# The tanh message-passing layer: gated vector products spread over three pipeline steps, with one more multiply on VectorE

## The reference, cut to what matters

```python
xs = concat([x[src, :8], x[dst, :8]])                   # 16 scalars of an edge
xv = concat([x[src, 8:], x[dst, 8:]]).reshape(E, 16, 3) # 16 vectors of an edge
h = sqrt(2) * relu(emb @ W1 / sqrt(10))
w = (h @ W2 / 4).reshape(E, 7, 16, 8)                   # per-edge weights
s_out, g_out = ...      # sums of xs and of the dots xv . n with w: 8 scalars, 8 gates
v_out = ...             # 8 vectors: xs x n with w, xv with w, and (xv, y2, W3J) with w
out = concat([1.593 * tanh(s_out), (1.593 * tanh(g_out))[:, :, None] * v_out]) * norm
return segment_sum(out, dst)
```

## Time and profile before

| | us |
|---|---|
| median of 3 runs | 14662.81 (14660.83 to 14662.97) |
| the profiled execution, its own time | 14665.89 |
| its span, first to last instruction | 14664.2 |
| PE busy in the span | 12078.2 (82%) |
| DVE busy | 12076.0 (82%) |
| POOL busy | 9995.6 (68%) |
| ACT busy | 7889.6 (54%) |

### The profile page before, as it was taken

The page is one execution under the profiler, slowest core; times in us unless marked ns, Lnnn a source line. Parts: engine busy times, 40 slices in busy tenths (PEclk is TensorE's granted clock), DMA queues, the critical chain, the costliest instruction groups (busy, mean ns, idle before and its releaser), DMA issues. The chain is left out here.

```text
span 14664.2 us, 437528 instructions
## 1 busy us (share of the span) xinstructions
PE 12078.2 (82%) x114342; PEld 9157.5 (62%) x114342; DVE 12076.0 (82%) x30182; ACT 7889.6 (54%) x23572; POOL 9995.6 (68%) x10550
## 2 busy tenths in 40 slices
PE   1555555555566999999999999988899999999999
PEld 1444444445455666666666666666677777777777
DVE  5777777777768999999999999986677777777776
ACT  0455555555544666666666666647544444444443
POOL 4777777777765666666666666637677777777775
PEclk8666666666668999999999999989899999999999
DMA  3555555555542222222222222218511111111111
GB/s 95 83 87 87 86 87 87 86 87 87 87 73 41 36 36 36 36 36 36 36 36 36 36 36 36 36 20 282 174 25 25 25 25 25 25 25 25 25 25 24
DMA packets 2705893, 840.24 MB, mean 57 GB/s; under 512 B 2232498, under 2 KB 2650073, under 8 KB 2704124
## 3 DMA queue, kind: packets, MB, share of 16 engines
q1 hardware_dynamic: 2212179, 616.76, 21.2%
q0 software_dynamic: 312320, 178.52, 9.3%
q10 hardware_dynamic: 181250, 43.25, 1.4%
HBM read 610.22 MB, written 226.58 MB: 57 GB/s over the span
## 5 line engine op out<-in xcount | busy, mean ns | idle before, releaser
L1401 POOL DMA_INDIRECT w_rows<-table,w_idx x9375 | 8949.5, 955 | 3848.0 <-issue 2539.0
L1384 PE MATMUL w_p_deg<-w_hot_lo,w_hot_row 128*128 128x196 bf16 x6250 | 1802.8, 336 | 1570.3 <-DVE w_hot_lo L1329 1512.1
L1637 PE MATMUL w_p_w<-w_w,w_ht 128*128 128x256 f32 x12500 | 3033.1, 390 | 0.0
L1637 PEld LDWEIGHTS w_p_w<-w_w,w_ht 128*128 128x128 f32 x12500 | 2272.7, 190 | 404.3 <-issue 0.2
L1869 DVE TENSOR_TENSOR w_prod<-w_p_xe,w_he 128x512 f32<-128x512 f32 x3125 | 2137.6, 684 | 4.1 <-PE w_p_xe L2012 4.1
L1619 ACT ACTIVATE w_ht<-w_p_h 128x512 f32<-128x512 f32 x1875 | 851.0, 526 | 2270.5 <-PE w_p_h L1651 2270.5
L1358 ACT CAST w_counts<-w_p_count 128x784 uint8<-128x784 f32 x1875 | 1247.7, 706 | 1451.8 <-PE w_p_count L1385 1442.0
L1384 PEld LDWEIGHTS w_p_deg<-w_hot_lo,w_hot_row 128*128 128x128 bf16 x6250 | 832.6, 133 | 1698.2 <-issue 1604.8
L1385 PE MATMUL w_p_count<-w_hot_lo,w_hot_row 128*128 128x196 bf16 x6250 | 1813.8, 337 | 0.0
L1147 ACT ACTIVATE w_dist<-row_iota,w_negrel 128x32 f32<-128x32 f32 x6250 | 1453.3, 309 | 301.0 <-issue 273.8
L2035 PE MATMUL w_p_sgt<-w_prod,w_wc 128*32 128x128 f32 x25000 | 1331.9, 284 | 85.4 <-ACT w_sgt L1948 64.1
(11 more groups left out here) (220 smaller groups left out, 20437.7 us busy)
## 6 DMA issues: line engine op xcount, KB each, us to landing
counts<-w_counts SPq DMA_DIRECT2D x1250, 122.5 KB
d_small<-counts SPq DMA_DIRECT2D x388, 392.0 KB
w_rows<-table,w_idx POOLq DMA_INDIRECT x9375
w_rel_row<-rel_row SPq DMA_DIRECT2D x625, 120.0 KB
w_edge<-e SPq DMA_DIRECT2D x625, 80.0 KB
w_idx<-src SPq DMA_DIRECT2D x1875, 2.5 KB
w_negrel<-negrel SPq DMA_DIRECT2D x1875, 2.5 KB
w_nodes<-split SPq DMA_DIRECT2D x1875, 2.0 KB
```

The lines of the kernel that those rows point to most:

```text
L1384: nc.tensor.matmul(p_deg[:], hot_row[s2][:, b, :], hot_lo[s2][:, b, :], start=False, stop=False, skip_group_check=True)
L1401: pool.indirect_dma_start(out=rows[:, t, :], out_offset=None, in_=table[0:N, :], in_offset=bass.IndirectOffsetOnAxis(ap=idx[:, t:t + 1], a ...
L1637: last = nc.tensor.matmul(p_w[(g.base * len(BANKS) + bank) % WBANKS][:, (t - t0) * 256:(t - t0 + 1) * 256], ht[g.slot(UNROLL)][:, k, t * P ...
```

## The change

The layer now uses `QuarterSums`. The gate is multiplied into the weights of both ends at once, straight out of PSUM (`gated_weights`), one step later than the tanh; the three products with the source vectors follow one by one in the same step, out of and into SBUF (`vector_products`), and `along` gets its own gated product (`along_products`). A step later the quarters are folded (`fold`, which holds the reduction over vectors that a wider reduction did before) and added. `DEPTH` goes from 5 to 6. `p_out` moves out of the PSUM bank of `p_rows` to one behind `p_wv`; `vector_weights` becomes one run of five matmuls. `dots` goes from POOL to DVE, and POOL's transfers no longer wait for tile products. ACT's order changes in two places. `window_sums` turns 72 instead of 64 columns.

```diff
-DEPTH = 5
+DEPTH = 6
-        w = WindowPass(nc, a, 1, sb, [p_low[0:MSG1, T * D:T * D + WIN]], MSG1)
-        p_out = p_low[:, T * D + WIN:T * (D + WIDE) + WIN].rearrange("p (t o) -> p t o", o=WIDE)
+        w = QuarterSums(nc, a, 1, sb, p_low[:, T * D:T * D + MIX], p_low[0:MSG1, T * D + MIX:T * D + MIX + WIN], MSG1)
+        p_ends = p_wv[:, 0:T * P].rearrange("p (t w c) -> p t w c", w=8, c=ENDS)
+        p_out = p_wv[:, T * P:T * (P + WIDE)].rearrange("p (t o) -> p t o", o=WIDE)
 # POOL
-                    nc.gpsimd.tensor_mul(dots[s2][:], v[:], spread(unit[s][:], [P, T, MUL1, 3], 2)).then_inc(dots_ready, 1)
-                    for t in range(T):
-                        wait_count(pool, prod_ready, g.times(T, t - 3 * T))
-                        pool.nop(nofuse=True)
-                        gather_tile(pool, a["table"][1], idx[s], rows[s], t, gathered[s])
+                    gather_rows(pool, a["table"][1], idx[s], rows[s], gathered[s])
 # DVE, new functions
+            def gated_weights(g):
+                vec.tensor_mul(gated[:], along[s2][:], gate[s2][:, :, 8:16]).then_inc(gated_ready, 1)
+                done(dve, wv_ready, g)
+                free(dve, w.mix_ready, g, 2)
+                vec.tensor_mul(mix[s2][:, :, :, 0:ENDS], p_ends, spread(gate[s2][:, :, 8:16], [P, T, 8, ENDS], 3)).then_inc(wv_used, 1)
+            def vector_products(g, k0, k1):
+                for k in range(k0, k1):
+                    vec.tensor_mul(to[:, :, :, 17 + 9 * k:25 + 9 * k], to[:, :, :, 0:8], spread(v16[s][:, :, 0:8, k], [P, T, 8, 8], 2))
+            def fold(g):
+                done(dve, w.mix_ready, g)
+                vec.tensor_copy(held[:, 0:72].rearrange("p (w c) -> p w c", c=9), p_mix[:, :, 0:9])
+                vec.tensor_reduce(held[:, 72:MSG1].rearrange("p (w k) -> p w k", k=3), p_mix[:, :, 9:OWN].rearrange("p w (k u) -> p w k u", u=9),
+                                  AX.X, ALU.add).then_inc(w.held_ready, 1)
...
 # ACT, end of a step
-                if g := at(3):
-                    done(act, wv_ready, g)
-                    nc.scalar.copy(wdst[g.slot(2)][:], p_dst).then_inc(wdst_ready, 1)
+                if g := at(3):
+                    free(act, out_ready, g, 2)
+                    activate(g, 0, 4)
                 if g := at(2):
                     done(act, xt_mm, g)
                     nc.scalar.copy(xt[g.slot(2)][0:SPLIT * 32, :], p_xt[:, 0:GE]).then_inc(xt_ready, 1)
-                if g := at(3):
-                    free(act, out_ready, g, 2)
-                    activate(g, 0, 4)
 # PE
                     expand(g, 0)
+                if g := at(6):
+                    w.sum_quarters(pe, g)
                 if g := at(4):
                     contract(g, 4)
...
                     last.then_inc(out_ready, 1)
                 if g := at(3):
                     contract(g, 0)
                     expand(g, 2)
-                    vector_weights(g, 0, 1)
                 if g := at(1):
-                    free(pe, gate_ready, g, 3)
-                    free(pe, vout_ready, g, 3)
+                    free(pe, w.acc_added, g, 5)
                     wg.product(pe, g)
...
                     contract(g, 1)
                     expand(g, 3)
-                    vector_weights(g, 1, 2)
+                if g := at(4):
+                    vector_weights(g)
+                if g := at(5):
+                    w.sum_edges(pe, g, lambda t: tile(g, t), lambda q: quarter(g, q))
+                if g := at(3):
                     contract(g, 2)
-                    vector_weights(g, 2, 3)
                     expand(g, 4)
-                    vector_weights(g, 3, T)
                     contract(g, 3)
                 if g := at(2):
                     done(pe, low_ready, g)
...
                     last.then_inc(xt_mm, 1)
-                if g := at(4):
-                    w.sum_window(pe, g, msg[g.slot(2)], msg_ready)
```

More of the change, by code:

```diff
@@ L57 @@
 SPLIT = 3
-SUM1, MSG1 = 64, 96
+MSG1 = 96
 EPS = 1e-5
@@ L1045, in _ @@
                     bank, at = j // 16, j % 16 * D
[L1046 removed]
+                    last = nc.tensor.matmul(p_part[:, c % 2, bank, at:at + D], nodes[64:MSG1, :, c * PJ + j], a["ident"][64:MSG1, 64:MSG1],
                                             start=True, stop=True)
@@ L1870, in tile_products, with gates @@
                                spread(he[g.slot(UNROLL)][:, t * P:(t + 1) * P], [P, 4, P], 1)).then_inc(prod_ready, 1)
[L1872 to L1878, removed]
+            def gates(g):
+                s2 = g.slot(2)
+                done(dve, bent_ready, g)
+                free(dve, gate_copied, g, 2)
+                vec.scalar_tensor_tensor(gate[s2][:], bent[s2][:], TANH_GAIN, spread(weight[g.slot(UNROLL)][:], [P, T, 16], 2),
+                                         ALU.mult, ALU.mult).then_inc(gate_ready, 1)
@@ L1970, in step @@
                     nc.scalar.activation(bent[s2][:], p_out[:, :, 0:G_ROWS], ACT.Tanh, scale=1.0 / 32 ** 0.5).then_inc(bent_ready, 1)
-                    done(act, gate_ready, g)
-                    free(act, w.acc_ready, g, 2)
-                    nc.scalar.copy(msg[s2][:, :, SUM1:SUM1 + 8], gate[s2][:, :, 0:8]).then_inc(gate_copied, 1)
+                    free(act, gated_ready, g, 2)
+                    nc.scalar.copy(along[s2][:], p_out[:, :, T_AT:SGT]).then_inc(along_ready, 1)
+                if g := at(1):
+                    s, s2 = g.slot(UNROLL), g.slot(2)
+                    done(act, wg.rows_ready, g)
+                    free(act, low_ready, g, 2)
+                    free(act, dots_ready, g, UNROLL)
+                    nc.scalar.copy(x32[s2][:, :, 8:16], p_rows[:, :, 0:8])
+                    nc.scalar.copy(v16[s][:, :, 8:16, :].rearrange("p t u k -> p t (u k)"), p_rows[:, :, 8:32]).then_inc(dst_copied, 1)
                 if g := at(2):
@@ L2014, in expand, with vector_weights, tile, quarter @@
                 last.then_inc(xe_ready, 1)
-            def vector_weights(g, t0, t1):
-                if t0 == 0:
-                    free(pe, wv_used, g, 1)
-                    free(pe, wdst_ready, g, 1)
-                for t in range(t0, t1):
-                    last = nc.tensor.matmul(p_wv[:, t * P:(t + 1) * P], he[g.slot(UNROLL)][:, t * P:(t + 1) * P], wv[:], start=True, stop=True)
-                if t1 == T:
-                    last.then_inc(wv_ready, 1)
+            def vector_weights(g):
+                done(pe, bent_ready, g)
+                done(pe, along_ready, g)
+                free(pe, wv_used, g, 1)
+                for t in range(T):
+                    last = nc.tensor.matmul(p_wv[:, t * P:(t + 1) * P], he[g.slot(UNROLL)][:, t * P:(t + 1) * P], wv[:], start=True, stop=True)
+                last.then_inc(wv_ready, 1)
+            def tile(g, t):
+                return mix[g.slot(2)][:, t, :, 8:SLOT]
+            def quarter(g, q):
+                return slice(2 * OWN * q, 2 * OWN * (q + 1)), mix[g.slot(2)][:, 4, 2 * q:2 * q + 2, 8:SLOT]
             def contract(g, t):
@@ L2046, in step @@
                     expand(g, 0)
+                if g := at(6):
+                    pe.wait_ge(dst_copied, g.times(1, 5) if at(2) else G)
+                    w.sum_quarters(pe, g)
                 if g := at(4):
@@ L2052, in step @@
                     done(pe, sgt_last, g)
-                    pe.wait_ge(dst_copied, g.times(1, 3) if at(2) else G)
-                    free(pe, w.acc_added, g, 1)
+                    free(pe, wv_used, g, 1)
                     for t in range(T):
```

135 lines of the change are left out of this document (65 added, 70 removed).

## The result

The changed kernel takes 14804.22 us (median of 4 runs, 14790.14 to 14809.33), the kernel before 14661.82: ratio 1.0096, 95% interval 1.0084 to 1.0109, or +142 us. The execution shown took 14790.14 us. The first row is the stretch of the earlier trace rows, the rest one step on TensorE (start, duration, work, idle time before it and what ended it), which answers to the earlier trace rows.

What follows compares the result with a forecast made beforehand. PE's in-order list, with its waits, was taken to bound the step. Terms summed to +0.28 us a step, times 625 +175, plus 4 for draining and final sums: 14842 us; own range 14750 to 14960, overall 14600 to 15010.

Steps and rivals of the forecast that it cites:

- 1 open time behind the transposes: From transposes to `expand` of tile 0 on PE: 1.05 us open instead of 0.95 filled by the window sum, +0.10.
- 2 the sums: New edge sums (0.51 and 0.25) and `sum_quarters` (0.22) are extra work on PE: +0.98 us a step, bounds 0.92 and 1.17.
- 3 `vector_weights`: Ten instructions in one run on PE take 1.25 us instead of 1.58 in four pieces: -0.33 a step.
- 4 the two waits: PE's waits for the gate (0.50) and ACT's copy of tiles 0 to 3 (0.18) go: -0.47 a step.
- 5 ahead of `p_out`: PE's wait ahead of `p_out` for ACT's copy of tile 4 stays: 0.
- idle stretch ahead of `expand` 0: Sign of being right: PE idle about 1 us there in every step, released by ACT's copy of the transposes.
- third rival: PE's clock falls for a tenth of the time, adding 0.7 us a step: 15280 us; chance 0.06.
- both their bounds: DVE products of 320 elements from SBUF were expected between 0.483 and 0.587 us.
- second rival: DVE sets the pace, its products and `dots` slowed beside POOL's transfers: +0.7 us a step, 15100 us; chance 0.09.
- faster rival: Waits gone are worth all the shown step shows, new matmuls at lower ends: -0.11 a step, 14598 us; chance 0.17.

Runs made afterwards that it cites:

- e4_fill_gap: Changed kernel plus five useless matmuls behind the transposes, whose result nobody reads; 14753.91 us, ratio 1.0061 to the kernel before.
- e9_sums_back: `e8_relu_first` with one edit: on TensorE `sum_edges` stands ahead of the transposes and no longer behind them; 15026.93 us, ratio 1.0246 to the kernel before.
- e7_before_one_run: Kernel before with its ten `vector_weights` instructions in one run behind `expand` 4 instead of four pieces; 14738.62 us, ratio 1.0051.
- e8_relu_first: Changed kernel with `sum_edges` behind the transposes, other work reordered, ScalarE's gathered-row copies at its step's end; 14393.26 us, ratio 0.9814 to the kernel before.
- e3_dots_pool: Changed kernel with the multiplication for the dots on GpSimd instead of VectorE; 14788.43 us, ratio 1.0085 to the kernel before.
- two tries: Changed kernel with `sum_edges` behind the transposes, fold and addition later: 14808.09 us; then with other work reordered on TensorE, VectorE and ScalarE: 15405.10 us.

## Why the prediction was right

Direction and size came out: 14842 forecast, 14804 measured, inside the forecast's own range. The size is in part luck, as the terms show. They are in us a step, as distances of starts on TensorE: means over all steps before, means over the steps outside the long ones after, so that the clock stands in a line of its own.

| term | forecast | measured |
|---|---|---|
| 1 open time behind the transposes | +0.10 | 1.385 against 1.280: +0.10 |
| 2 the sums | +0.98 | 0.509 + 0.125 + 0.244: +0.88 |
| 3 `vector_weights` | -0.33 | 1.263 against 1.588 (first piece at 0.30): -0.32 |
| 4 the two waits | -0.47 | gate -0.29, copy 0.532 less 0.327, -0.20: -0.49 |
| 5 ahead of `p_out` | 0 | 0.472 against 0.489: -0.02 |
| not foreseen: `sum_quarters` and not a contraction straight behind `expand` 0 | | 0.236 against 0.327: -0.09 |
| not foreseen: contraction 3 and not a piece straight behind `expand` 4 | | 0.327 against 0.223: +0.10 |
| not foreseen: contraction 2 to `expand` 4 | | 0.334 against 0.356: -0.02 |
| the long steps, left out of the sum | | 8.627 - 8.550: +0.08 |

The lines add up to +0.22, and the steps themselves differ by 0.217, which over 625 is 135 us. The five terms alone give +0.15 where the forecast had +0.28. That the time came within 38 us of the forecast is owed to the clock, which the sum put at nothing: `e4_fill_gap`, where it doesn't fall, takes 14754, which is 88 below the forecast and at the low end of its own range of 14750 to 14960.

- Term 1: right. The idle stretch ahead of `expand` 0 and its releaser are as foretold; `e9_sums_back` shows the price of this open time in another order of the work, 0.65 a step.
- Term 2 was mis-sized, below its own lower bound of 0.92: the fifth tile's part, taken unscaled at 0.25, takes 0.125, and `sum_edges` 0.63 where the forecast named 0.7 to 0.8 as a sign of being right.
- Terms 3 and 4 are right only together. Each was costed as if it stood alone; `e7_before_one_run` shows that the first piece of `vector_weights` lay in the gate's wait, so that its 0.30 became a gain only because the wait went too.
- The wait for the copy in term 4 was read against a free `expand` of 0.23. Straight in front of a contraction it takes 0.327 without any wait (`e8_relu_first`, `e9_sums_back`), so that 0.09 of what went there was no wait for the copy. The same 0.10 came back at `expand` 4, where a piece of `vector_weights` had stood between the `expand` and the contraction.
- The clock: the third rival came true in part, at a ninth of its price (48 us, against 15280 - 14842 = 438), with a granted clock of 0.99 in the stretch. That it belongs to the standing still is shown by `e4_fill_gap`.
- VectorE: its load fell from 8.00 to 4140.73 / 521.5 = 7.94 a step, just short of the 0.1 to 0.5 expected. The large instructions did as foretold: 3.51 went and 3 x 0.593 + 0.820 + 0.399 = 3.00 came, although the products of 320 elements, at 0.593, lie above both their bounds. The small ones were mis-sized: 0.374 + 0.282 = 0.66 went, and 0.193 + 0.361 + 0.233 + 0.373 = 1.16 came. `e3_dots_pool` shows that the load did not matter.
- The second rival needed products that take twice as long beside GpSimd's transfers. From 5000 to 9400 us 88 of 1527 products lay wholly inside a transfer; they took 0.612 in the mean, the others 0.592. The Trainium skill, "GPSIMD Engine Reference", section Specifications, says that GpSimd shares its SBUF interfaces with VectorE and that instructions with two SBUF inputs contend for them. The trace shows at most 0.02 us of it in a product.
- The faster rival needed `vector_weights`, both sums and the waits to be 0.28 cheaper together than forecast; they were 0.11 cheaper. (It lies 65 us below the median of 14662.81, not 67.)

## What to carry to other kernels

Before moving work out of a place, ask what wait it covered. In the kernel before, 0.95 us of sums stood behind the transposes, where TensorE would have waited for ScalarE's copy anyway. In `e8_relu_first` 0.63 us of sums stand there again; one place earlier (`e9_sums_back`) the same sums add 1.02 us to a step. Moving them back pays only if each engine's queue is followed: two tries ended at a copy or an addition that stood in front of something urgent, and the third, with one pair of copies moved, gained 1012 us on the second. An instruction taken out of a wait, as in the run of `vector_weights`, saves nothing until the wait goes. And a forecast that comes out should be checked term by term: here an error of -0.13 us a step in the five terms and one of +0.08, the clock, made it look better than it was.

## What the runs showed of the hardware that I had not expected

- In the changed kernel TensorE stops for 0.88 to 0.96 us once in each step of some 8.5, and the granted clock fell 35 times from 1.00 to 0.50 in the pass. With the stop filled with useless matmuls it fell no time, and the kernel was 50 us faster. In `e7_before_one_run` it fell 13 times, each time after a stop of 0.65 to 0.71; in the kernel before, with three stops over 0.5 in the whole pass, it didn't fall.
- A VectorE product of 320 f32 elements shows 0.593 us from two SBUF operands and 0.587 from one in PSUM, and in both the next instruction starts about 0.50 after it. Another product of 320 from two SBUF operands, in another arrangement, takes 0.483; which part the arrangement has in this is not shown.
- A contraction (f32, 32 weight columns) that stands straight behind an `expand` (bf16, 128 columns) starts 0.33 us after it wherever nothing is waited for (in the changed kernel and in `e7_before_one_run`, `e8_relu_first` and `e9_sums_back`); where `sum_quarters`, the row product or `vector_weights` stands behind the `expand`, that one starts after 0.22 to 0.24. The profile shows no idle time and no releaser for the 0.10, and what makes it stays open.
